# Loading and splitting the next stage's rows and weights in the stage before it, and moving five waits for stores to their readers

## The reference, cut to what matters

```python
xn  = layernorm(x)                                   # x: 4 x 1024 x 256
s   = causal_attention(xn, 16 heads of 16) @ W_o.T
for l in range(2):                                   # u starts as xn
    h = shift_token(u); q, k, v = split(h @ wqkv[l])
    q, k = rotary_xpos(l2norm(q) * q_scale, l2norm(k) * k_scale)
    u = u + local_attention(q, k, v, window 128) @ wo[l]
    h = layernorm(shift_token(u)) * ln_g + ln_b
    a, g = split(h @ w1[l] + b1[l])
    u = u + (a * gelu(g)) @ w2[l] + b2[l]
out = x + s * silu(u)
```

## Time and profile before

| | us |
|---|---|
| median of 3 runs | 2039.32 (2033.78 to 2041.57) |
| the profiled execution, its own time | 2041.56 |
| span of the trace in it | 2039.8 |
| granted TensorE clock, mean | 0.954 of full |
| PE busy | 1858.8 (91%) |
| DVE, ACT, POOL busy | 1520.4, 1219.0, 974.1 |
| HBM read, written | 82.41 MB, 41.96 MB |

### The profile page before, as it was taken

One profiled execution on the slowest core, in us unless ns is written; L12 is line 12 of the kernel. 1 busy time (PEld: TensorE's weight loads), 2 busy tenths in 40 slices (PEclk: granted clock), 3 DMA queues, 4 the chain that ended last, 5 costly groups with the idle time before them and its releaser, 6 DMA issues. The chain is left out here.

```text
span 2039.8 us, 39803 instructions
## 1 busy us (share of the span) xinstructions
PE 1858.8 (91%) x12960; PEld 1332.7 (65%) x12960; DVE 1520.4 (75%) x4148; ACT 1219.0 (60%) x2522; POOL 974.1 (48%) x804
## 2 busy tenths in 40 slices
PE   5869999999996899999996999879999999689998
PEld 4633333333331688888885788758888888578787
DVE  5657888888881899999995554279999999655553
ACT  3414666666665577777774434257887887544443
POOL 3441222222222577777771434257777777244333
PEclk9867999999998899999997999979999999799999
DMA  5792564464432000000022121110000002222212
GB/s 198 240 187 34 69 82 64 65 83 67 62 48 68 8 27 26 26 26 26 26 70 67 32 62 52 53 55 27 26 26 26 26 26 70 57 67 83 82 53 83
DMA packets 142258, 126.27 MB, mean 62 GB/s; under 512 B 31090, under 2 KB 124718, under 8 KB 141998
## 3 DMA queue, kind: packets, MB, share of 16 engines
q1 hardware_dynamic: 140782, 123.36, 26.5%
q10 hardware_dynamic: 1344, 1.31, 0.2%
HBM read 82.41 MB, written 41.96 MB: 61 GB/s over the span
## 5 line engine op out<-in xcount | busy, mean ns | idle before, releaser
L636 ACT ACTIVATE ca_pr<-ca_pS 128x1024 f32<-128x1024 f32 (+3 forms) x384 | 296.6, 811 | 211.6 <-PE ca_pS L550 169.9
L470 POOL TENSOR_SCALAR_AFFINE_SELECT ca_pr<-ca_pr 128x256 f32<-128x256 f32 x256 | 103.2, 406 | 389.4 <-ACT ca_pr L636 385.2
L662 DVE CUSTOM_DVE_ANT_0 ca_masked<-ca_pR,ca_later 128x256 f32<-128x256 f32 (+3 forms) x512 | 235.6, 485 | 42.5 <-PE ca_pR L526 39.4
L526 PE MATMUL ca_pR<-ca_ks,ca_qs 96*128 96x512 bf16 (+3 forms) x768 | 220.6, 346 | 18.1 <-DVEq L719 14.6
L666 DVE TENSOR_REDUCE ca_mx<-ca_pR 128x1 f32<-128x512 f32 x256 | 175.7, 686 | 29.9 <-PE ca_pR L526 28.0
L550 PE MATMUL ca_pS<-ca_qs,ca_ks 98*128 98x512 bf16 (+3 forms) x768 | 184.0, 330 | 9.8 <-issue 3.5
L526 PEld LDWEIGHTS ca_pR<-ca_ks,ca_qs 96*128 96x128 bf16 x768 | 70.6, 98 | 173.8 <-DVE ca_mx L662 89.8
L895 ACT ACTIVATE w_pe<-w_sm,w_nmax 128x256 f32<-128x256 f32 x256 | 126.7, 496 | 69.6 <-DVE w_nmax L1007 69.6
L571 PE MATMUL ca_pO<-ca_pr,ca_va 128*32 128x512 f32 (+3 forms) x1536 | 164.5, 500 | 1.6 <-POOL ca_pr L470 0.8
L826 POOL TENSOR_TENSOR w_tsn<-w_qk,w_tab 128x512 f32<-128x512 f32 x62 | 127.4, 2074 | 79.1 <-DVE w_pn L1016 79.1
L826 POOL TENSOR_TENSOR wb_tsn<-wb_qk,wb_tab 128x512 f32<-128x512 f32 x62 | 127.3, 2070 | 79.3 <-DVE wb_pn L1016 79.3
(11 more groups left out here) (268 smaller groups left out, 5446.4 us busy)
## 6 DMA issues: line engine op xcount, KB each, us to landing
QKP<-p_parts SPq DMA_DIRECT2D x32, 384.0 KB, 2.9
ca_qs<-QKP SPq DMA_DIRECT2D x96, 128.0 KB, 6.7
ca_ks<-QKP SPq DMA_DIRECT2D x96, 128.0 KB, 7.1
f_hh<-X SPq DMA_DIRECT2D x32, 256.0 KB, 5.3
p_xin<-x SPq DMA_DIRECT2D x8, 512.0 KB, 5.4
X<-p_xn SPq DMA_DIRECT2D x8, 512.0 KB, 4.1
VA<-p_vst SPq DMA_DIRECT2D x8, 512.0 KB, 3.5
ca_vin<-VA SPq DMA_DIRECT2D x16, 256.0 KB, 10.0
```

What stands on the lines that cost most here:

```text
L526: pe.matmul(bank[:, 0:w], qs[0:SHIFT_ROW, u, h, i * P:(i + 1) * P], ks[0:SHIFT_ROW, u, h, k0:k0 + w], start=True, stop=True).then_inc(ring ...
L636: act.activation(pr[:, k % 2, pair, :, 0:w], pS[:, pair, :, 0:w], ACT.Exp, scale=CS).then_inc(p_ready, 1)
L662: dve.tensor_tensor_reduce(masked[:, jb % RING, 0:w], pR[jb % RING][:, 0:w], later[:, 512 - w:512], -1.0, BIG, ALU.add, ALU.min, mx[:, i, ...
```

## The change

- The constants' block goes; its work lies at the head of the projection block. There the x loads are now issued first and the rotary tables behind them. POOL also does in its `first`, ahead of the first group's L198: masks, the presets of the causal stage, and the start values of 99 semaphores (`K.starts`), which stood in the causal stage.
- The projection's loops are written out. `moments(s + 2)` and `rstd_of(s + 2)` lie after the third group of step s; before, `moments(s + 1)` opened step s. SP stores xn and loads x after the second group, for the next step. The 13 stack transfers of group 0 are issued in four turns behind steps 2 to 5; before, behind the groups of step 6.
- The waits for the last stores at a block's end go. The reader waits instead: `load` in the causal stage for q, k and v, SP at the head of window 1 for X, `phase_feed` for x1, the closing for the attention output.
- Rows and wqkv of layer 0 are loaded at the start of the causal stage and split in iterations 4, 5 and 6 (ACT after the output copy at k = 4, POOL ahead of the diagonal at k = 8). Those of layer 1 are loaded in steps 1 and 3 of feed 0 and split in its last two steps.
- The feed stage's first steps (constants, split of w1, norm, transposes, high and low part of super tile 0) lie in the last two tiles of the window stage. The split of w2 moves from ahead of the first gelu to the middle of step 0 (ACT) and behind its fifth chunk (DVE).
- To make room, several tensors now live longer or are shared: `big_*` serves the projection too.

```diff
-def phase_project(nc, K, x, X, QKP, VA, wqk, wv):
+def phase_project(nc, K, W, x, X, QKP, VA, wqk, wv):
...
+            def rows_of(s, j):
+                store_xn(s, j, s // 2)
+                if s + 2 < SUPERS:
+                    sp.dma_start(xin[:, j], x_t[s + 2]).then_inc(x_loaded[j], 16)
...
             for j in range(2):
                 sp.wait_ge(xn_stored[j], ONE + 16 * SUPERS // 2)
-                sp.wait_ge(v_stored[j], ONE + 16 * SUPERS // 2)
-            for g in range(CG):
-                sp.wait_ge(part_stored[g], ONE + 16 * SUPERS)
...
             def first():
                 rstd_of(0, 0)
+                rstd_of(1, 1)
+                window_masks()
+                causal_presets()
+                for t, n in K.starts:
+                    pool.sem_inc(t, n)
...
+                    if g == CG - 2 and s + 2 < SUPERS:
+                        moments(s + 2, j, it + 1)
...
             def load(n, u):
+
+                xn_stored, part_stored, v_stored = K.stored
+                sp.wait_ge(part_stored[n % CG], ONE + (n // CG + 1) * 2 * 16)
+                for i in range(2):
+                    sp.wait_ge(v_stored[i], ONE + (n // CG + 1) * 16)
...
                 for n in range(1, SLOTS):
                     load(n, n)
+                load_rows(sp, W, 0, X)
+                load_qkv(sp, W, 0, wqkv)
                 place_shift(0, NJ + NEARLY + 1)
...
+                    if i == len(DIAGONAL) // 2 and 0 <= n - SPLIT_AT < 3:
+                        split_qkv(pool, W, 0, n - SPLIT_AT)
...
-            for half in range(2):
-                sp.wait_ge(att_stored[half], ONE + ITERS * 16)
...
                 exps(w, j, it, 0)
                 exps(w, j, it, 1)
+                if late == 0:
+                    feed_weights(0)
...
                 normalise(w, j, it, 1)
+                if late == 1:
+                    feed_normalise()
...
+                if late == 0:
+                    feed_moments()
+                elif late == 1:
+                    feed_lo()
...
-            for i in range(2):
-                sp.wait_ge(S["x1_stored"][i], ONE + (layer + 1) * (NW // 2) * 16)
-            sp.sem_inc(K.passed, 1)
...
+                if s == 1:
+                    load_qkv(sp, W, layer + 1, wqkv)
+                elif s == 3:
+                    sp.wait_ge(S["x2_stored"][0], ONE + (layer * (NS // 2) + 1) * 16)
+                    load_rows(sp, W, layer + 1, X)
...
+                if not closing and s == L:
+                    act.wait_ge(S["g_ready"], ONE + (g0 + NS) * HC)
+                    for z in range(3):
+                        qkv_high(act, W, layer + 1, z)
```

More of the change, by code:

```diff
@@ L129, in steps @@
             first()
[L130 to L134, removed]
+            for s in range(SUPERS):
+                step(s, s % 2, s // 2, s == SUPERS - 1)
         @block.sync
@@ new lines, in window_masks @@
+            def window_masks():
+                pool.memset(K.masks[:, :, :], 0.0).then_inc(masked, 1)
+                pool.wait_ge(masked, ONE + 1)
+                m = K.masks[:, :, :].rearrange("p m (s t) -> p m s t", s=2)
+                for kind in range(3):
+                    own = kind // 2
+                    pool.affine_select(out=m[:, kind, own], in_=m[:, kind, own], compare_op=ALU.is_ge, fill=NEG,
+                                       base=0, pattern=[[-1, P]], channel_multiplier=1).then_inc(masked, 1)
+                    prev = m[:, kind, 1 - own]
+                    if kind:
+                        pool.affine_select(out=prev, in_=prev, compare_op=ALU.is_ge, fill=NEG,
+                                           base=0, pattern=[[1, P]], channel_multiplier=-1).then_inc(masked, 1)
+                    else:
+                        pool.memset(prev, NEG).then_inc(masked, 1)
@@ L336, in _, with phase_causal @@
             steps(pe, first, step)
-def phase_causal(nc, K, QKP, VA, AO):
+def phase_causal(nc, K, W, X, QKP, VA, AO, wqkv):
     ITERS = BATCH * CG
@@ L357, in phase_causal @@
     SPREAD_AT = 2
+    SPLIT_AT = 4
     RJ = NJ + 3
@@ L729, in load_h, with chunks_of, phase_window @@
           .then_inc(F.sems["h_loaded"][j], 16)
+def chunks_of(w, part):
+    if part == 2:
+        return w[:, :, TAIL_COL:TAIL_COL + P]
+    half = slice(3 * P * part, (3, WHOLE)[part] * P)
+    return w[:, :, 0:TAIL_COL].rearrange("p k (z c) -> p k z c", z=2)[:, :, :, half]
 def score_place(h):
     return 2 * (h // 4) + h % 2, h // 2 % 2
-def phase_window(nc, K, W, F, layer, X, wqkv, wo, qk_scales, w1):
+def phase_window(nc, K, W, F, layer, X, wqkv, wo, qk_scales, w1, ln_g, ln_b, b1):
     NW = TILES
@@ L1220, in _, with phase_feed @@
             steps(pe, step)
-def phase_feed(nc, K, W, F, layer, X, ln_g, ln_b, b1, w2, b2, AO, x, woc, out):
+def phase_feed(nc, K, W, F, layer, X, wqkv, w2, b2, AO, x, woc, out):
     NS = SUPERS
@@ L1416, in _ @@
         def _(act):
-            act.wait_ge(S["w1_loaded"], ONE + (layer + 1) * 4 * 16)
-            for part in range(3):
-                act.activation(chunks_of(w1_hi, part), chunks_of(w1_st, part), ACT.Copy).then_inc(S["w_hi"], 1)
             def turned(s, j):
@@ L1559, in residual @@
                         tail_low(s + 1, 1 - j)
+                    if not closing and s == L - 1 and n:
+                        split_qkv(dve, W, layer + 1, n - 1)
                     if closing and s == L and n == SUP - 1:
```

371 lines of the change are left out of this document (217 added, 154 removed).

## The result

| | us | ratio to the kernel before |
|---|---|---|
| kernel before, median | 2036.68 (4 runs, 2033.78 to 2041.57) | |
| changed kernel, median | 1989.26 (4 runs, 1988.02 to 1995.32) | 0.9765 (95%: 0.9741 to 0.979) |
| forecast | 1992, range 1976 to 2009 | |

What follows compares the result with a forecast made beforehand. PE is busy for 91% of the span, so only its waits or lower clock can be won back. Start, projection, seams and losses sum to 47.0 us: 1994.6 for the profiled execution, 1992 for a median, range 1976 to 2009.

Steps and rivals of the forecast that it cites:

- Start: Kernel start: x load issued some 1.85 us earlier without the constants' block and tables ahead; gain 2.2 us, bounds 1.5 and 3.
- Projection: Projection's 8 steps: statistics and rstd made a step ahead shorten steps to 11.5 us; 98.4 against 106.8, gain 8.4 us.
- rival 1: Projection flows at 10.3 us a step and the queue does not hold the shift: about 1979 us; chance 0.20.
- POOL's hold: Projection: POOL sets 99 semaphores ahead of its first part, so step 1's ACT waits for the buffer; 5.2 us lost.
- Start of the causal stage: Up to first scores: maxima start earlier, but the shift lands no earlier behind queued loads; 0 us, bounds -2 and +4.3.
- Causal stage, window seams: Splits in iterations 4 to 6 cost 1 us; causal to window 0 gains 11.6, feed 0 to window 1 gains 12.2.
- Window to feed: Window to feed seams: first w1 product earlier as norm and splits move ahead; gains 7.3 in layer 0, 6.8 in layer 1.
- Feed stages: Each feed stage: 2 us lost in step 0 by w2's copy and subtraction, 0.5 by loads; -2.5 each.
- 2: Rival: projection gains nothing, with DMA full and POOL's late first part rippling on; causal start loses 2; about 2003; chance 0.20.
- 3: Rival: table product behind wo and scales sets the window prologue, 1 to 3 us less per layer's seam; 1999; chance 0.05.
- 4: Rival: slower, as PE's clock stays at 0.50 behind the first scores; 2070 for three iterations; chance 0.05, 0.03 of it slower.
- 5: Rival: a moved reader's wait holds SP's queue as the old one did, at the load of groups; counted in 2.

Runs made afterwards that it cites:

- first profile: First profiled execution of the changed kernel, nothing edited: 1988.55 us, span 1986.7.
- hold_early: Changed kernel with POOL's masks and presets ahead of the first variance and the 99 start values between the first and second: span 1983.7 us.
- stacks_late: Changed kernel with group 0's 13 transfers issued behind steps 6 and 7 in place of 2 to 5: span 2001.8 us.
- shift_first: Changed kernel with layer 0's rows and wqkv loaded behind the first shift transfers: span 1991.4 us.
- ends_waited: Changed kernel with the five waits for last stores back at the blocks' ends: span 1995.3 us.
- second profile: Profile of the changed kernel run again, nothing edited: span 1989.0 us; median of its 5 runs 1990.84 us.
- qkv_later: Changed kernel with the three wqkv loads in feed 0 behind step 2's row loads, not ahead: span 1989.5 us.
- w2_early: Changed kernel with ACT copying w2's high part behind its first chunk and DVE subtracting ahead of chunk 2: span 1981.7 us.
- combined: Changed kernel with hold_early, shift_first, qkv_later, w2_early and the table product waiting for scales alone, squares ahead of v's copy: 1973.31 us, ratio 0.9685.

## Why the prediction was right, and where its steps were off

The time was 2.7 us under the forecast, and at most seams the mechanism was the one named. That the total came so near is partly luck: in the first profile the terms that gave more than forecast are 12.5 us over, and those that gave less 6.4 under. The misses:

- **Start, 2.2 forecast, 3.1 and 3.2 measured.** The issue is 1.85 us earlier, as said. The first x load also lands faster than I counted without the tables ahead of it: statistics start at 4.61, for 5.4.
- **Projection, 8.4 forecast, 11.5 and 12.4 measured.** Two terms were mis-sized, against each other. Undisturbed steps take 10.6 us, not 11.5: I let the rest of the gap lower the clock, and it does not (0.80 us idle at a clock of 1.00). That is rival 1's flow. The Trainium skill (TensorE: Matmul & The Clock Gate, What's actually happening) says that the throttled state is the default and that activity releases it; these rows agree with that. The chain that I added up to 5.0 gives 4.9. POOL's hold was taken at 5.2 and cost 6.85 (hold_early). POOL's first part was forecast for 29.7 and came at 29.2, and its store freed ACT at 33.3 for 33.5; but ACT wanted the buffer at 26.3, not 28.3, so it waited for 7.0. That the last step gets shorter as group 0's transfers leave it is in no term. The 2 us for queued stores were 2.1 (11.4 + 11.5 + 11.0 less three steps of 10.6), and went with stacks_late.
- **Start of the causal stage, 0 forecast, 3.9 and 3.0 measured.** The step that failed is "the loads of groups 1 and 2 still wait for the v store's landing". The reader's wait counts only the stores of its own batch, which landed long before; the loads are issued 1.0 us behind the last v store, where I had them 4.4 to 4.9 behind it. The loads then begin 2.0 us behind the last part's end, where I had 5.0 to 5.5, and most of the maxima's 4.4 us was kept. That the shift is held by the loads ahead of it was right (0.7 to 2.6 us, shift_first), and rival 1's "not held" was wrong. But the hold is far too small to take back 4.4 us. The Trainium skill (DMA: Bandwidth & Descriptors, Queues, rings and completion order) has ring order in the first half of what the prediction quotes. These traces agree: in all ten with loads ahead, the scores come 0.2 to 0.5 us behind the last load's landing, and an overtaking showed in none.
- **Causal stage, window seams.** The splits in iterations 4 to 6 were taken at 1 us; the stage is 0.3 and 0.6 longer. At the seams it is 10.0 and 10.4 for 10.4 and 11.2 in the first profile: wo's load and the table product are the next late, as said. The landing waits were worth 1.7 and 1.9 (ends_waited), where I had the blocks start 1.7 and 2.5 earlier.
- **Window to feed.** First cosines to first w1 product gained 12.4 and 12.3, in the second profile 10.6 and 12.0, for 10.5 and 10.3. The product comes 2.9 us behind the residual, not 4.
- **Feed stages, -2.5 each forecast, -6.2 and -4.0 measured.** "DMA is mostly idle there" was true and beside the point: 1.57 MB ahead of one row load made it late, and this and the clock behind it cost 2.5 (qkv_later). The place of w2's split costs some 0.5 us in layer 0 and up to 2.6 in layer 1 (w2_early; 0.3 to 0.5 and 1.7 to 1.8 by combined), where 2 each were forecast. Of feed 0's loss some 3 us are left in combined: the steps from its last low part on take 1.6 longer, where wqkv is split (no run tests that this is the cause), and step 1 takes 1.5 longer for a cause that I didn't find.
- **Rivals.** Of 1, the steps of 10.6 us came true and the free shift didn't. 2 and 3 didn't happen: the late first part rippled through one more step only (11.9), and the table product was in the sum already. 4, the clock staying low behind the first scores, didn't either: 8 us at 0.50, 0.77 in the next 4 and then 1.00, as before. Its 2070 for three iterations at half clock would be 2082 by its own 30 us each. 5 was wrong for the reason given above, since no load waits there. Of the signs named, first scores at 41 to 43 us behind the last part and the first w1 product 4 us behind `w_x` did not show (37.7 and 38.5, 2.9).

## What to carry to other kernels

When a wait for stores moves from a block's end to its reader, read which count the reader waits for: a reader of an older batch doesn't wait at all, which was worth 3.4 us at the first maxima (ends_waited). Work without data, such as setting semaphores, costs what it holds up: 99 of them with some masks, ahead of a step's first group, cost 7 us, and nothing in gaps of the same engine a few us earlier. A bulk load that is not urgent goes behind the small ones that are, even on an idle DMA; the two places where it stood ahead of them here cost 0.7 to 2.6 and 2.5 us.

## What the runs showed of the hardware that I had not expected

- A gap on PE of the same length, 3.1 to 3.2 us, at the same place of the program, is followed by full clock in three profiles and by 0.6 to 0.8 over 8 us in eleven; this makes up to 3.7 us of difference. Near the end of the causal stage the same small gaps (1.2 and 0.9 us) brought half clock in eleven profiles and none in three.
- A transfer of 8 KB behind 2.4 MB of queued loads took from 3.4 to 5.4 us to its reader in ten profiles, and 2.74 to 2.76 in the four in which no load landed later than 1.9 us behind its issue: the queue adds spread as well as time, and both by when the last load lands.
- Stores of 384 KB landed after 5.2 us in the median in place of 2.9, and the projection was still faster. Beside group 0's transfers (50 to 95 us) it is 6.3, and 3.4 in stacks_late: ACT waits for them by 0.7 to 1.4 us in three steps, and these take only 0.4 to 0.9 us more.
